# A recommendation-model tower: half grams in two bursts, with transposes and layers between them, and a new order of ScalarE's work

## The chip, the core and the metric

The kernel runs on one core of a Trainium2 chip. Times are device microseconds of one execution of the program; lower is better. The engines of the core work in parallel and wait for one another by semaphores: TensorE (PE; PEld is its weight load), VectorE (DVE), ScalarE (ACT), GpSimd (POOL) and SyncE (SP), which here only issues transfers. DMA engines move the data.

## The reference

A batch of 512 samples looks up 26 embedding rows of 128 numbers each. With the dense vector that makes 27 vectors for each sample. All 351 products of two different vectors, and the dense vector itself, go through three layers.

```python
e = jnp.stack([tbl_0[ids[:, 0]], ..., tbl_25[ids[:, 25]]], axis=1)
T = jnp.concatenate([dense[:, None, :], embs], axis=1)
Z = jnp.einsum('bnd,bmd->bnm', T, T)
z = Z[:, iu0, iu1]                                  # pairs n < m
h = jnp.concatenate([z, r_dense], axis=1)           # 351 + 128 = 479
h = jnp.maximum(h @ W_top1 + b_top1, 0.0)           # 512
h = jnp.maximum(h @ W_top2 + b_top2, 0.0)           # 256
y = h @ W_top3                                      # 1
```

## The kernel before

**Lookups.** Twelve small tables are read whole and looked up on TensorE: for each chunk of 128 table rows a one-hot matrix `hot` (128x512) is made, and two matmuls (with `t_hi`, the table rounded, and `t_lo`, the rest) add the chunk's rows into a PSUM bank. Tables 0 to 5 have 8 chunks and tables 6 to 11 have 10, 108 in all, numbered by k. ScalarE casts `t_hi` (`high_part`), VectorE subtracts for `t_lo` (`low_part`, in the middle of the chunks of the table before). VectorE makes four of five `hot`, ScalarE each fifth (`one_hot`, from `apart`, the distances computed ahead). There are 8 `hot` buffers and three of `t_hi` and `t_lo`: the cast of table i+2 has to wait until TensorE is through with table i-1. ScalarE also copies each finished bank into `XT` (`copy_lookups`). The other 14 fields are gathered row by row by GpSimd (56 gathers, held back by counts of TensorE's progress in `row_turn`), turned on TensorE into two PSUM banks `tp` (steps "rows" t, g; four groups of up to four fields for each tile t) and copied into `XT` by ScalarE.

**Grams.** The batch is cut into four tiles of 128 samples. For each tile there are two half grams of 64 samples: 32 small matmuls (two records each in the trace) into one of two halves of PSUM. VectorE and ScalarE copy each half out: `copy_low` (twice each, into `Zlow`, which lies in `table`'s space) and `copy_high` (twice each, four copies apiece, into `Zt`). The third half has to wait until the first is copied out by both engines (`gram_dve`, `gram_act`), and so on. When both halves of a tile are in `Zlow`, six transfers move parts of it to other partitions of `Zt` (`low_stars`, four of them, and two small ones), and the semaphore `low_in` of the tile tells that they have landed.

**Layers.** "dense" and "layer1" of a tile are 4 and 12 matmuls; layer1 waits for the copies and for `low_in`. VectorE makes `h1` of it, then layer2 follows. Tile 3 is last and has layouts of its own; there GpSimd issues three of the moves.

The order of all of it is written out by hand in `timeline()`. TensorE, ScalarE and VectorE all walk this one list `STEPS`; each takes the kinds that it has work for.

Of the kernel before, what the change touches and what calls it, by code (L numbers as in the profile page):

```python
# [27 lines left out]
P = 128  # L28
BATCH = 512
TILES = BATCH // P  # L30
# [32 lines left out]
ROWS_AFTER = {3: [(0, 0), (0, 1)], 5: [(0, 2), (0, 3)], 7: [(1, 0)], 8: [(1, 1)], 10: [(1, 2)], 11: [(1, 3)]}  # L63
# [16 lines left out]
MOVES = QUADS + SMALL  # L80
SHARED_MOVES = 3
# [19 lines left out]
def timeline():  # L101

    steps = []
    for i in range(K_OH):
        steps.append(("onehot", 0, i))
        steps += [("rows", t, g) for t, g in ROWS_AFTER.get(i, [])]
    steps += [("gram", 0, 0), ("gram", 0, 1), ("rows", 2, 0), ("gram", 1, 0), ("gram", 1, 1), ("rows", 2, 1),
              ("dense", 0, 0), ("layer1", 0, 0), ("layer1", 0, 1), ("rows", 2, 2), ("layer2", 0, 0), ("rows", 2, 3),  # L110
              ("gram", 2, 0), ("gram", 2, 1), ("dense", 1, 0), ("layer1", 1, 0), ("layer1", 1, 1),
              ("rows", 3, 0), ("rows", 3, 1), ("rows", 3, 2), ("dense", 2, 0), ("layer1", 2, 0), ("layer1", 2, 1),
              ("rows", 3, 3), ("gram", 3, 0), ("gram", 3, 1), ("layer2", 1, 0), ("layer2", 2, 0), ("dense", 3, 0),
              ("layer1", 3, 0), ("layer2", 3, 0), ("turn", 0, 0), ("layer3", 3, 0)]
    return steps
# [59 lines left out]
def dlrm_tower(nc, dense, ids, ids_oh, tbls, small, w1, w2, tail, ends, out):  # L175
    f32, f32r, i32 = mybir.dt.float32, mybir.dt.float32r, mybir.dt.int32
    ALU, ACT = mybir.AluOpType, mybir.ActivationFunctionType
    with ExitStack() as ctx:
# [99 lines left out]
        def _(sp):  # L278
# [27 lines left out]
            for t in range(TILES):  # L306
                low_stars(sp, t, range(QUADS - (SHARED_MOVES if t == TILES - 1 else 0)), low_in[t])
# [45 lines left out]
        def _(pe):  # L353
# [14 lines left out]

            pe.wait_ge(ident_ready, 1)
            for _ in range(WARM_UP):  # L370
                nc.tensor.transpose(l1[:, 0, :], ident[:], ident[:])
            for kind, t, i in STEPS:
# [30 lines left out]
                elif kind == "gram":  # L403
# [6 lines left out]
                    if t == 1 and i == 0:  # L410
                        pe.wait_ge(lookup_copied, K_OH)
# [3 lines left out]
                    for q in range(QH):  # L415
                        for s in range(0, SAMPLES, COUPLE):
                            b = t * P + (i * SAMPLES + s) * QH + COUPLE * q
                            last = nc.tensor.matmul(gr[PAD * s:PAD * s + COUPLED, halves % HALVES, q, 0:COUPLE * FIELDS],  # L418
                                                    XT[:, b:b + COUPLE, :].rearrange("d s n -> d (s n)")[:, 0:COUPLED],
                                                    XT[:, b:b + COUPLE, 1:PLACES], start=True, stop=True)  # L420
# [322 lines left out]
```

## Time and profile before

| | before |
|---|---|
| median of 3 runs (lowest to highest) | 116.45 us (116.12 to 116.63) |
| the profiled execution: its time | 116.73 us |
| its span in the trace | 114.9 us |
| busy: PE, PEld, DVE, ACT, POOL | 102.7, 87.2, 79.3, 78.6, 70.4 us |
| shares of the chain that ended last: PE, DMA, SP's queue, issue, DVE, ACT | 58, 9, 9, 9, 8, 6% |

How to read it: the busy time of an engine is a sum over stages, so the share says little by itself. Starts are given from the span's start. For TensorE the distance from start to start is what counts, since its records overlap. A bracket at the end of a row tells how long the engine idled ahead of it and what ended that. The 1.83 us between the execution's time and its span lie outside the trace.

### The profile page before, as it was taken

The page shows a single profiled execution, that of the slowest core. Times are in us where ns is not written, and L with a number is a line of the kernel's source. Part 1 is how long each engine was busy: PE and PEld are TensorE (multiplying, and loading weights), DVE is VectorE, ACT ScalarE, POOL GpSimd, SP SyncE. Part 2 cuts the span into 40 slices and gives each one's busy share as a digit, 9 for nine tenths or more (in the row PEclk, how much of TensorE's full clock was granted, in tenths as well). Part 3 has the DMA queues.
Part 4 walks back from the last instruction along what each step waited for, and adds up shares of the span by engine and source line. Part 5 has one row for each costly group of instructions (what it writes and reads, how often), then busy time and mean ns, then how long its engine had stood idle before and what let it go on. Part 6 is the DMA issues. An engine that isn't in the chain of part 4 may idle for free.

```text
span 114.9 us, 2626 instructions
## 1 busy us (share of the span) xinstructions
PE 102.7 (89%) x981; PEld 87.2 (76%) x981; DVE 79.3 (69%) x202; ACT 78.6 (68%) x169; POOL 70.4 (61%) x68
## 2 busy tenths in 40 slices
PE   4999779999929999999999987897889987899993
PEld 4976456888627888888888877887779976798990
DVE  5497999999196989999999109994227920269531
ACT  4284999999791999999996249998217860168011
POOL 7477786878771377887878776777777600005000
PEclk9999999999995999999999999999999999999999
DMA  2879999998892659982010221232222210000000
GB/s 88 237 263 391 380 382 387 385 328 251 267 273 86 185 200 160 377 282 56 7 39 23 58 56 51 57 86 59 53 70 56 59 36 0 0 6 18 9 0 1
DMA packets 7413, 16.44 MB, mean 143 GB/s; under 512 B 2124, under 2 KB 3048, under 8 KB 7272
## 3 DMA queue, kind: packets, MB, share of 16 engines
q1 hardware_dynamic: 5368, 12.36, 32.7%
q0 software_dynamic: 1888, 3.71, 11.1%
q10 hardware_dynamic: 144, 0.20, 0.5%
q8 instruction: 8, 0.13, 0.5%
q14 instruction: 5, 0.04, 0.1%
HBM read 16.02 MB, written 0.00 MB: 139 GB/s over the span
## 4 chain that ended last, share of the span: by engine, by line
PE 58%; DMA 9%; SPq 9%; issue 9%; DVE 8%; ACT 6%; ACTq 0%; DVEq 0%
PE work L397 17%; PE work L399 17%; PE work L364 6%; DMA ids_bc<-ids_oh 6%; SPq L274 5%; PE work L457 5%; PE work L418 5%; PE tp L383 4%; DMA Zt<-table 3%; DVE Zt L499 3%; DVE table L491 3%; ACT t_hi L512 2%; ACT apart L529 2%; SPq L295 2%; PE work L467 2%
## 5 line engine op out<-in xcount | busy, mean ns | idle before, releaser
L347 POOL DMA_INDIRECT rows<-tbl,idx x56 | 66.7, 1190 | 22.0 <-issue 14.3
L397 PE MATMUL work<-hot,t_hi 128*128 128x512 f32 x108 | 44.1, 408 | 3.9 <-DVE hot L651 3.0
L399 PE MATMUL work<-hot,t_lo 128*128 128x512 f32 x108 | 42.9, 397 | 0.0
L651 DVE TENSOR_SCALAR hot<-ids_bc,rownum 128x512 fp32r<-128x512 int32 x87 | 36.5, 482 | 3.0 <-PE work L399 2.0
L397 PEld LDWEIGHTS work<-hot,t_hi 128*128 128x128 f32 x108 | 20.6, 191 | 11.2 <-DVE hot L651 5.1
L399 PEld LDWEIGHTS work<-hot,t_lo 128*128 128x128 f32 x108 | 20.7, 191 | 3.7
L622 DVE TENSOR_TENSOR t_lo<-table,t_hi 128x1280 fp32r<-128x1280 f32 (+3 forms) x14 | 16.6, 1183 | 4.9 <-ACT t_hi L512 4.6
L593 ACT COPY XT<-tp 128x512 f32<-128x512 f32 (+1 forms) x16 | 9.8, 639 | 12.5 <-PE tp L383 12.5
L529 ACT ACTIVATE apart<-ids_bc,minus_row 128x512 f32<-128x512 int32 x21 | 15.0, 716 | 3.2 <-DMA ids_bc<-ids_oh 3.2
L418 PE MATMUL work<-XT 128*58 128x52 f32 x512 | 14.7, 217 | 2.4 <-DVE Zt L499 1.0
L418 PEld LDWEIGHTS work<-XT 128*58 128x58 f32 x512 | 14.1, 133 | 3.4 <-issue 2.0
L512 ACT CAST t_hi<-table 128x1280 fp32r<-128x1280 f32 (+3 forms) x14 | 14.1, 1009 | 1.7 <-DMA table<-small 1.7
L539 ACT ACTIVATE hot<-apart 128x512 fp32r<-128x512 f32 x21 | 13.3, 636 | 0.9 <-PE work L399 0.8
L499 DVE COPY Zt<-work 17x48 f32<-17x48 f32 (+1 forms) x64 | 12.8, 201 | 1.0
L499 ACT COPY Zt<-work 17x48 f32<-17x48 f32 (+1 forms) x64 | 12.5, 195 | 0.8
L491 DVE COPY table<-work 14x224 f32<-14x224 f32 x16 | 6.1, 381 | 9.3 <-PE work L418 7.3
L551 ACT COPY XT<-work 128x512 f32<-128x512 f32 x11 | 12.2, 1107 | 0.0
L364 PE MATMUL work<-Zt,w_sb 128*128 128x128 f32 x84 | 10.2, 277 | 1.6 <-DMA Zt<-table 1.6
L364 PEld LDWEIGHTS work<-Zt,w_sb 128*128 128x128 f32 x84 | 9.7, 192 | 2.0 <-issue 2.0
L491 ACT COPY table<-work 14x224 f32<-14x224 f32 x16 | 5.7, 356 | 5.8 <-PE work L418 3.4
L274 POOL DMA_DIRECT2D Zt<-table x3 | 1.6, 535 | 12.9 <-DVE table L491 12.9
L383 PE MATMUL tp<-ident,rows 128*128 128x128 f32 x56 | 8.9, 287 | 0.4 <-ACT XT L593 0.4
(44 smaller groups left out, 59.6 us busy)
## 6 DMA issues: line engine op xcount, KB each, us to landing
table<-small SPq DMA_DIRECT2D x6, 640.0 KB, 6.4
ids_bc<-ids_oh SPq DMA_DIRECT2D x12, 256.0 KB, 5.6
table<-small SPq DMA_DIRECT2D x4, 512.0 KB, 9.2
w_sb<-w SPq DMA_DIRECT2D x1, 1024.0 KB, 7.4
rows<-tbl,idx POOLq DMA_INDIRECT x56, 5.5
table<-small SPq DMA_DIRECT2D x2, 320.0 KB, 5.2
w_sb<-w SPq DMA_DIRECT2D x1, 512.0 KB, 8.8
dense_t<-dense SPq DMA_DIRECT2D x1, 256.0 KB, 9.0
```

The lines of the kernel that those rows point to most:

```text
L347: nc.gpsimd.indirect_dma_start(rows[:, t, place - FIRST, :], None, tbls[f], bass.IndirectOffsetOnAxis(ap=idx[:, t, place - FIRST:place - F ...
L364: last = nc.tensor.matmul(l1_block(t, u), w1_sb[:, c, u * P:(u + 1) * P], Zt[:, t, c, :], start=False, stop=c == CHUNKS - 1 and (t == TILE ...
L383: last = nc.tensor.transpose(tp[:, bank, j * P:(j + 1) * P], rows[:, t, a + j - FIRST, :], ident[:])
L397: nc.tensor.matmul(bank, t_hi[:, i % PARTS, c * D:(c + 1) * D], hot[:, k % HOTS, :], start=c == 0, stop=False)
L399: last = nc.tensor.matmul(bank, t_lo[:, i % PARTS, c * D:(c + 1) * D], hot[:, k % HOTS, :], start=False, stop=c == n - 1)
L418: last = nc.tensor.matmul(gr[PAD * s:PAD * s + COUPLED, halves % HALVES, q, 0:COUPLE * FIELDS], XT[:, b:b + COUPLE, :].rearrange("d s n -> ...
L491: return copy(Zlow[:, t % 2, :, first:end:COUPLE], gr[PAD * s:PAD * s + LOW, half, :, column(s):column(s) + LOW].rearrange("n q m -> n m q"))
L499: last = copy(Zt[PAD * g:PAD * g + n, t, :, first:end:COUPLE], gr[PAD * s:PAD * s + n, half, :, column(s) + n - CHUNKS:column(s) + n].rear ...
L512: nc.scalar.copy(t_hi[:, i % PARTS, c0 * D:c1 * D], table[:, i % TABLES, c0 * D:c1 * D]).then_inc(hi_ready, 1)
L529: nc.scalar.activation(apart[:, j % 2, :], ids_bc[:, i % IDS, :], ACT.Abs, bias=minus_row[:, KINDS.index(OH_CHUNKS[i]), c:c + 1]).then_inc ...
L622: nc.vector.tensor_tensor(t_lo[:, i % PARTS, c0 * D:c1 * D], table[:, i % TABLES, c0 * D:c1 * D], t_hi[:, i % PARTS, c0 * D:c1 * D].bitcas ...
L651: nc.vector.tensor_scalar(hot[:, k % HOTS, :], ids_bc[:, i % IDS, :], rownum[:, v, c:c + 1], None, ALU.is_equal).then_inc(hot_dve, 1)
```

## The change

- Each half gram is cut into a "burst" (the first 16 of its matmuls) and "gram" (the other 16, which also tells that the half is full). For tiles 0 to 2, transposes of rows, a tile's dense part, or half a layer1 stand between the two.
- The whole order behind the lookups is new. Rows are turned later among the lookups: one group behind each of tables 4 to 9 instead of up to two behind tables 3, 5, 7, 8, 10 and 11. All of tile 2's rows are turned before tile 1's last half; layer2 of tile 1 stands before tile 3's rows.
- In ScalarE's list the cast of `t_hi` for table i+2 stands first in step i (for tables 0 and 1 behind one `hot`), ahead of the `hot` and the copy of the bank.
- For tiles 0 to 2 two of the four `low_stars` transfers are issued by ScalarE, between its two high copies of the tile's second half; SyncE issues the other two and the two small ones.

```diff
-ROWS_AFTER = {3: [(0, 0), (0, 1)], 5: [(0, 2), (0, 3)], 7: [(1, 0)], 8: [(1, 1)], 10: [(1, 2)], 11: [(1, 3)]}
+ROWS_AFTER = {4: [(0, 0)], 5: [(0, 1)], 6: [(0, 2)], 7: [(0, 3)], 8: [(1, 0)], 9: [(1, 1)]}
+SCALAR_MOVES = 2
...
-                low_stars(sp, t, range(QUADS - (SHARED_MOVES if t == TILES - 1 else 0)), low_in[t])
+                low_stars(sp, t, range(QUADS - (SHARED_MOVES if t == TILES - 1 else SCALAR_MOVES)), low_in[t])
...
+            def couples(t, i, half, first, end):
+
+                for q in range(first, end):
+                    for s in range(0, SAMPLES, COUPLE):
+                        b = t * P + (i * SAMPLES + s) * QH + COUPLE * q
+                        last = nc.tensor.matmul(gr[PAD * s:PAD * s + COUPLED, half, q, 0:COUPLE * FIELDS],
...
-                elif kind == "gram":
+                elif kind == "burst":
                     pe.wait_ge(tp_empty, banks_filled(("rows", t, len(GROUPS) - 1)))
...
+                    couples(t, i, halves % HALVES, 0, QH // 2)
+                elif kind == "gram":
+                    couples(t, i, halves % HALVES, QH // 2, QH).then_inc(gram_full, 1)
                     halves += 1
...
-                    for n, k in enumerate(mine_in(i)[1:]):
+                    rest = mine_in(i)[1:]
+                    if rest and i < HEADED:
+                        one_hot(rest[0])
+                    if i + 2 < K_OH:
+                        high_part(i + 2, 0, OH_CHUNKS[i + 2])
+                    if rest and i >= HEADED:
+                        one_hot(rest[0])
+                    if i:
+                        copy_lookups(i - 1)
+                    for k in rest[1:]:
                         one_hot(k)
...
                     if i + 1 < K_OH:
                         one_hot(mine_in(i + 1)[0])
-                    if i + 2 < K_OH:
-                        high_part(i + 2, 0, OH_CHUNKS[i + 2])
...
+                    if t < TILES - 1 and i == 1:
+                        low_stars(nc.scalar, t, range(QUADS - SCALAR_MOVES, QUADS), low_in[t])
```

ScalarE's list around table 4, before. `table_in5` and `table_in6` mark the casts of tables 5 and 6; the `hot` between them are the eighth of table 4 and the fifth of table 5:

```order
L512 CAST t_hi<-table 128x1024 [waits hot_used,table_in5]
L593 COPY XT<-tp 128x128x4 [waits tp_full] x2
L539 ACTIVATE hot<-apart 128x512 [waits hot_used,apart_ready]
L529 ACTIVATE apart<-ids_bc,minus_row 128x512 [waits hot_act,rownum_ready,ids_in5]
L551 COPY XT<-work 128x512 [waits hot_used]
L539 ACTIVATE hot<-apart 128x512 [waits hot_used,apart_ready]
L529 ACTIVATE apart<-ids_bc,minus_row 128x512 [waits hot_act,rownum_ready,ids_in6]
L512 CAST t_hi<-table 128x1280 [waits hot_used,table_in6]
```

The same place now:

```order
L520 CAST t_hi<-table 128x1280 [waits hot_used,table_in6]
L547 ACTIVATE hot<-apart 128x512 [waits hot_used,apart_ready]
L537 ACTIVATE apart<-ids_bc,minus_row 128x512 [waits hot_act,rownum_ready,ids_in5]
L559 COPY XT<-work 128x512 [waits hot_used]
L547 ACTIVATE hot<-apart 128x512 [waits hot_used,apart_ready]
L537 ACTIVATE apart<-ids_bc,minus_row 128x512 [waits hot_act,rownum_ready,ids_in6]
L606 COPY XT<-tp 128x128x4 [waits tp_full]
L520 CAST t_hi<-table 128x1280 [waits hot_used,table_in7]
```

The cast of table 6 moved ahead of two `hot`, two `apart` and the copy of a bank, and the next cast now stands right behind a copy of turned rows.

TensorE's list behind the last lookup, before:

```order
L418 MATMUL work<-XT 58x52 [waits dense_copied,last_copied,xt_ready,lookup_copied,tp_empty]
L418 MATMUL work<-XT 58x52 x31
L418 MATMUL work<-XT 58x52 [waits tp_empty]
L418 MATMUL work<-XT 58x52 x31
L383 MATMUL tp<-ident,rows 128x128 [waits rows_in2_0,tp_empty]
L383 MATMUL tp<-ident,rows 128x128 x3
L418 MATMUL work<-XT 58x52 [waits gram_dve,gram_act,lookup_copied,tp_empty]
L418 MATMUL work<-XT 58x52 x31
L418 MATMUL work<-XT 58x52 [waits gram_act,gram_dve,tp_empty]
L418 MATMUL work<-XT 58x52 x31
```

And now, from the burst of tile 0's second half to the burst of tile 1's second:

```order
L377 MATMUL work<-XT 58x52 x16
L361 MATMUL work<-dense_t,w1_sb 128x128 [waits dense_in,w1_in,lookup_copied]
L361 MATMUL work<-dense_t,w1_sb 128x128 x3
L377 MATMUL work<-XT 58x52 [waits gram_act,gram_dve,tp_empty]
L377 MATMUL work<-XT 58x52 x15
L396 MATMUL tp<-ident,rows 128x128 [waits rows_in2_1,tp_empty]
L396 MATMUL tp<-ident,rows 128x128 x3
L377 MATMUL work<-XT 58x52 x16
L396 MATMUL tp<-ident,rows 128x128 [waits rows_in2_2,tp_empty]
L396 MATMUL tp<-ident,rows 128x128 x3
L377 MATMUL work<-XT 58x52 [waits gram_act,gram_dve,tp_empty]
L377 MATMUL work<-XT 58x52 x15
```

The dense part and the groups of rows moved in between the halves and into them; the fourth half still waits for the second to be copied out.

ScalarE's list at tile 0's second half gram, before (`table` is `Zlow`):

```order
L491 COPY table<-work 14x14x16 x2
L499 COPY Zt<-work 17x3x16
L499 COPY Zt<-work 20x3x16
L499 COPY Zt<-work 23x3x16
L499 COPY Zt<-work 26x3x16
```

and now, with the two copies of turned rows that stand ahead of it and the two transfers behind the first high copy:

```order
L606 COPY XT<-tp 128x128x2
L606 COPY XT<-tp 128x128x4
L499 COPY table<-work 14x14x16 x2
L507 COPY Zt<-work 17x3x16
L507 COPY Zt<-work 20x3x16
L507 COPY Zt<-work 23x3x16
L507 COPY Zt<-work 26x3x16
L277 DMA Zt<-table 8x384
L277 DMA Zt<-table 5x384
```

The second high copy, four more copies, moved behind two issues.

## Rows read from the trace of the kernel before

**Rows 1.** Timeline of TensorE around table 5's end: start, duration, instruction, [idle before].

```profile
33.74 0.66 PE L397 MATMUL work<-hot,t_hi 128*128 128x512 f32 x1 [2.21 <-DVE hot L651]
...
37.40 0.48 PE L397 MATMUL work<-hot,t_hi 128*128 128x512 f32 x1
```

**Rows 2.** Timeline of ScalarE and VectorE ahead of that.

```profile
30.51 1.25 ACT L512 CAST t_hi<-table 128x1280 fp32r<-128x1280 f32 x1
...
31.79 1.49 DVE L622 TENSOR_TENSOR t_lo<-table,t_hi 128x1280 fp32r<-128x1280 f32 x1 [2.57 <-ACT t_hi L512]
```

**Rows 3.** Busy times by stretch: the granted clock (PEclk) behind that gap.

```profile
core 0: us, PE busy (x) PEld busy (x) DVE busy (x) ACT busy (x) POOL busy (x), PEclk, DMA share, GB/s
...
33.00:36.00 3.00, 2.26 (x6) 1.78 (x7) 2.66 (x7) 1.89 (x3) 1.19 (x1) 0.65 0.69 262
```

**Rows 4.** Timeline of TensorE: table 8's first and seventh chunk, table 9's first.

```profile
46.94 0.48 PE L397 MATMUL work<-hot,t_hi 128*128 128x512 f32 x1
...
49.77 0.39 PE L397 MATMUL work<-hot,t_hi 128*128 128x512 f32 x1
...
51.95 0.48 PE L397 MATMUL work<-hot,t_hi 128*128 128x512 f32 x1
```

**Rows 5.** Timeline of ScalarE in the same place.

```profile
46.15 1.25 ACT L512 CAST t_hi<-table 128x1280 fp32r<-128x1280 f32 x1
47.31 0.71 ACT L593 COPY XT<-tp 128x512 f32<-128x512 f32 x1
47.89 0.62 ACT L539 ACTIVATE hot<-apart 128x512 fp32r<-128x512 f32 x1
```

**Rows 6.** DMA issues from 12.4 to 12.8 us (table 6): size, us to landing.

```profile
table<-small SPq DMA_DIRECT2D x1, 640.0 KB, 9.9
```

**Rows 7.** Timeline of GpSimd's gathers where one waits for TensorE.

```profile
39.74 1.16 POOL L347 DMA_INDIRECT rows<-tbl,idx  x1 [1.87 <-PE work L399]
```

**Rows 8.** Timeline of TensorE behind the lookups.

```profile
66.92 3.62 PE L418 MATMUL work<-XT 128*58 128x52 f32 x128 [0.43 <-issue]
70.47 0.66 PE L383 MATMUL tp<-ident,rows 128*128 128x128 f32 x4
...
82.14 1.97 PE L457 MATMUL work<-w_sb,apart 128*128 128x256 f32 x8 [0.44 <-issue]
83.94 0.38 PE L383 MATMUL tp<-ident,rows 128*128 128x128 f32 x2
...
88.34 1.16 PE L358 MATMUL work<-dense_t,w_sb 128*128 128x128 f32 x8
89.33 2.84 PE L364 MATMUL work<-Zt,w_sb 128*128 128x128 f32 x24
92.01 1.04 PE L383 MATMUL tp<-ident,rows 128*128 128x128 f32 x8
...
99.34 3.62 PE L418 MATMUL work<-XT 128*58 128x52 f32 x128 [0.47 <-ACT XT L593]
...
107.49 1.57 PE L364 MATMUL tp<-Zt,w_sb 128*128 128x128 f32 x12
```

**Rows 9.** Timeline of ScalarE: its copies of the first half gram.

```profile
68.93 0.74 ACT L491 COPY table<-work 14x224 f32<-14x224 f32 x2 [1.35 <-PE work L418]
69.70 1.64 ACT L499 COPY Zt<-work 17x48 f32<-17x48 f32 x8
```

**Rows 10.** The chain that ended last, from 90 to 95.7 us: start, us, what.

```profile
90.16 0.83 SPq L274
...
91.86 0.66 SPq L274
...
92.57 0.71 SPq L274
...
93.91 1.69 DMA Zt<-table
```

**Rows 11.** Timeline of SyncE's issues for tile 3.

```profile
103.83 0.83 SPq L274 DMA_DIRECT2D Zt<-table  x1
104.71 1.17 SPq L309 DMA_DIRECT2D Zt<-table  x2
```

**Rows 12.** Timeline of the first issues on two queues.

```profile
0.74 0.38 ACTq L553 DMA_DIRECT2D table<-small  x1
...
0.74 0.42 SPq L286 DMA_DIRECT2D idx<-ids  x1
```

More of the change, by code:

```diff
@@ L108, in timeline @@
         steps += [("rows", t, g) for t, g in ROWS_AFTER.get(i, [])]
[L109 to L114, printed above, removed]
+    steps += [("burst", 0, 0), ("rows", 1, 2), ("gram", 0, 0), ("rows", 1, 3), ("burst", 0, 1), ("rows", 2, 0),
+              ("gram", 0, 1), ("dense", 0, 0), ("burst", 1, 0), ("rows", 2, 1), ("gram", 1, 0), ("rows", 2, 2),
+              ("burst", 1, 1), ("rows", 2, 3), ("gram", 1, 1), ("layer1", 0, 0), ("layer1", 0, 1), ("layer2", 0, 0),
+              ("burst", 2, 0), ("dense", 1, 0), ("gram", 2, 0), ("layer1", 1, 0), ("burst", 2, 1), ("layer1", 1, 1),
+              ("gram", 2, 1), ("layer2", 1, 0), ("rows", 3, 0), ("rows", 3, 1), ("dense", 2, 0), ("rows", 3, 2),
+              ("layer1", 2, 0), ("layer1", 2, 1), ("rows", 3, 3), ("burst", 3, 0), ("gram", 3, 0), ("burst", 3, 1),
+              ("gram", 3, 1), ("layer2", 2, 0), ("dense", 3, 0), ("layer1", 3, 0), ("layer2", 3, 0), ("turn", 0, 0),
+              ("layer3", 3, 0)]
     return steps
@@ L367, in from_pairs @@
                 return last
+            def couples(t, i, half, first, end):
[3 more added lines that the diff above has]
+                        last = nc.tensor.matmul(gr[PAD * s:PAD * s + COUPLED, half, q, 0:COUPLE * FIELDS],
+                                                XT[:, b:b + COUPLE, :].rearrange("d s n -> d (s n)")[:, 0:COUPLED],
+                                                XT[:, b:b + COUPLE, 1:PLACES], start=True, stop=True)
+                return last
             pe.wait_ge(ident_ready, 1)
@@ L409, in _ @@
                         pe.wait_ge(xt_ready, 1)
-                    if t == 1 and i == 0:
-                        pe.wait_ge(lookup_copied, K_OH)
                     if halves >= HALVES:
@@ L414, in _ @@
                         pe.wait_ge(gram_act, halves - HALVES + 1)
[L415 to L420, printed above, removed]
-                    last.then_inc(gram_full, 1)
+                    couples(t, i, halves % HALVES, 0, QH // 2)
+                elif kind == "gram":
+                    couples(t, i, halves % HALVES, QH // 2, QH).then_inc(gram_full, 1)
                     halves += 1
@@ L424, in _ @@
                     if t == 0:
+                        pe.wait_ge(lookup_copied, K_OH)
                         pe.wait_ge(w1_in, 16)
@@ L562, in _ @@
                 if kind == "onehot":
-                    for n, k in enumerate(mine_in(i)[1:]):
+                    rest = mine_in(i)[1:]
[8 more added lines that the diff above has]
+                    for k in rest[1:]:
                         one_hot(k)
-                        if n == 0 and i:
-                            copy_lookups(i - 1)
-                    if i and len(mine_in(i)) < 2:
-                        copy_lookups(i - 1)
                     if i + 1 < K_OH:
                         one_hot(mine_in(i + 1)[0])
-                    if i + 2 < K_OH:
-                        high_part(i + 2, 0, OH_CHUNKS[i + 2])
                     if i == K_OH - 1:
```

## The prediction

> **What bounds the kernel now.** I read the page first (TensorE has by far the most busy time), then TensorE's timeline for its gaps, then the timelines of the engines that ended them, and the chain that ended last for the stretch behind the lookups. TensorE runs nearly without a break from 19 to 66 us, except once: it idles 2.21 us ahead of table 5's sixth chunk [rows 1]. VectorE had waited 2.57 us for the cast of table 6 before it could go on to `t_lo` and that chunk's `hot`; ScalarE only began the cast at 30.51 [rows 2]. Behind the gap the granted clock is 0.65 over 33 to 36 us [rows 3], so part of that stretch ran at the lower of TensorE's two levels (1.2 instead of 2.4 GHz) after the engine had idled. Behind the lookups TensorE alternates grams, transposes and layers with gaps under 1 us, each set by a copy or by the moves into `Zt`.
>
> **The gap among the lookups goes.** In the new list the cast of table 6 waits only for TensorE to end table 3 (24.5 us) and for the table itself, issued at 12.4 and 9.9 us later there, at 22.3 [rows 6]. So it ends near 26.2, before VectorE wants it (near 28.9). What the gap cost: TensorE would have issued the next matmul at 31.37 and did at 33.74, 2.37 us. From there to 37.40 are 3.66 us [rows 1] for three chunks and six transposes. A table of ten chunks with four transposes takes 5.01 us [rows 4] and four transposes about 0.45 (70.47 to the end of a group in rows 8; eight are 1.04 busy), so a chunk is 0.456 and the stretch should be 1.37 + 0.66 = 2.03 us: 1.63 lost at the low level. Together 4.0 us.
>
> **Two things take part of it back.** First, with the transposes behind table 3 gone, TensorE wants table 4's sixth chunk sooner, and VectorE, which has just made a `t_lo`, is about 0.25 us late. Second, ScalarE now does, behind each of tables 5 to 9: copy of the turned rows, cast, then the `hot` of the next table's seventh chunk. By rows 5 that is 0.58 + 1.16 + 0.62 from a start at 0.37 behind the table's first matmul (47.31 against 46.94): ready at 2.73. The chunk's matmul starts at 49.77 - 46.94 = 2.83 [rows 4, 5], its weight load 0.2 ahead. That is no slack at all; I take 0.1 us for each of five tables. So the same work among the lookups ends 4.0 - 0.25 - 0.5 = 3.25 us sooner. One group of transposes (0.45) also moves behind the lookups: the last lookup ends at 62.3 and not at 66.06, and the first burst starts at 63.15 instead of 66.92 [rows 8]. GpSimd's gathers follow: the one that waited 1.87 us for TensorE [rows 7] waits for table 6's first group of chunks, now near 34.8, so all later gathers shift some 3.8 us with it and the rows are there in time.
>
> **Behind the lookups.** Prices [rows 8], start to start: a half gram 3.55 / 2 = 1.78, so a burst 0.9; four transposes 0.45, two 0.22; dense 1.0 (88.34 to 89.33); layer1 2.68 (to 92.01), half of it 1.35; layer2 1.8 (82.14 to 83.94). ScalarE's copies of a half take 0.77 + 1.64 = 2.4 us and start 0.2 behind its last matmul [rows 9]; a copy of turned rows is 0.6 [rows 5].
> ScalarE's walk: half (0,0) is full at 65.4 and copied at 68.0; two row copies to 68.9; half (0,1): low until 69.7, first high until 70.5, then the second high has to wait for the two issues.
> *Price of an issue on ScalarE.* The trace has none behind compute. The same two transfers cost SyncE 0.66 and 0.71 with 0.04 between [rows 10], 1.42 in all. Lower bound: they are hidden, 0. Upper: nothing is hidden, 1.45. They only wait for the low copies, and four high copies (0.82, half of rows 9) stand between; I take it that the queue issues while these run, so 0.65 is exposed. That lies near the middle, and both ends stay in the range.
> So (0,1) is copied at 72.0. TensorE, from 63.15: burst, 4 transposes, gram, 2 transposes, burst, 4 transposes, gram, dense (68.9), burst, 4, gram, 4 (71.6); the burst of (1,1) waits for ScalarE until 72.1; burst, 2 transposes, gram (74.15). Tile 0's moves: SyncE now has four issues instead of six, which takes 1.45 from the 5.44 us between the low copy's end and landing (90.16 to 95.60 [rows 10]): 69.75 + 4.0 = 73.75, in time. Layer1 of tile 0 to 76.85; `h1` costs 1.04 with no cover any more (rows (2,2) filled 0.45 of it); layer2 to 79.7. Then burst, dense, gram, half layer1, burst, half layer1, gram: 7.3, to 87.0; layer2 of tile 1 to 88.95; 8 transposes and dense to 90.85; 4 transposes, 91.35. Tile 2's moves: low copies end 88.0, landed 92.0. Layer1 of tile 2 from 92.15 to 94.85, where it was 95.74 + 2.7 before. Two transposes and their copy, 0.9: tile 3's grams start at 95.75 instead of 99.34. Change: 3.6 us.
>
> **Tile 3.** Before, 8.15 us from there to layer1 (107.49) [rows 8], filled by two layer2. Now one of them (1.8) has gone ahead, but that gives nothing: tile 3's moves are issued at 103.83 and 104.71 for 1.17 [rows 11]; the last of them starts near 105.3 and lands no sooner than the 1.7 us of rows 10 later, at 107.0, so layer1 can't start before 7.7 us after the grams. TensorE will idle about 1.8 us there: the gap that layer2 covered comes open. I keep 8.15; 7.7 would be 0.4 less.
>
> **Sum.** 3.6 us sooner, less 0.3 for a dozen more changes of the kind of work on TensorE, which rows 8 show to cost little but not nothing: 3.3. On the profiled execution 116.73 - 3.3 = 113.4; the median of the runs is 0.28 below it, so **113.2 us**. Its own range is 112.5 to 114.1.
>
> **A rule on the issues.** The Trainium skill, Perfetto Trace Analysis, section DMA Instruction — HWDGE (DVE, Sync), says that the block that generates descriptors is shared and locked for exclusive use during an issue. By it SyncE's and ScalarE's issues would queue behind one another, and the first rival below would come out, at 115.7. But two queues issue at the same moment, in 0.38 and 0.42 us [rows 12], each no longer than alone, which speaks against it for these sizes.
>
> **Rivals.**
> - *ScalarE's issues take turns with SyncE's.* ScalarE is then held for four issues, about 2.85 us instead of 1.42. (0,1) is copied at 73.4, the burst of (1,1) starts 1.4 later; the six issues are in one row again, tile 2's moves land 5.44 and not 4.0 behind the low copies. Sum: 1.4 + 1.4 of the 3.6 are lost: 116.45 - 0.8 = 115.7. Against it: [rows 12]. 12%.
> - *The issues on ScalarE are hidden.* Another 0.65 off, and up to 0.4 in tile 3: 112.3. 13%.
> - *The clock falls again.* TensorE idles 1.8 us before the last layer1 and about 1 us in three other places. 2.21 us of idling went ahead of a fall [rows 1, 3], gaps of 0.4 did not [rows 8]; between them nothing is known. Price as above, 1.63: 114.8. 14%.
> - *Slower than before: ScalarE's list becomes the bound in the lookups.* Rows copy, cast and `hot` are a closed loop with TensorE (the transposes at a table's end release the copy). I gave it 0.1 us a table. If the `hot` comes 0.75 late in each of five tables, 3.3 us are gone and the kernel is at 116.5 or above; a fall of the clock in such gaps would do it at less. For: the loop has no slack. Against: its parts are all measured, 2.73 against 2.83. 8%; within 0.5% by a partial miss 5%.
> - The forecast 48%.
>
> Range: from the hidden issues to the shared generator, **112.1 to 115.7**. A measurement can tell about 0.5% (0.6 us) from no change: faster by more 0.86, within it 0.06, slower 0.08.
>
> **What would show it.** TensorE without a gap over 0.5 us between 20 and 62, the granted clock at full there, the last lookup's end near 62.3; ScalarE's second high copy starting 0.6 us behind the first in half (0,1); layer1 of tile 2 near 92; tile 3's grams near 96 and its layer1 8 us later with TensorE idle ahead of it. Wrong if a new gap ahead of each table's seventh chunk stands in TensorE's timeline, if ScalarE's issues are longer than 0.75 us, or if the clock is low behind 90 us.

## The result, and the profile after

| | before | after |
|---|---|---|
| median (lowest to highest), 4 runs each | 116.28 us (116.03 to 116.63) | 115.09 us (114.55 to 115.36) |
| the profiled execution: time, span | 116.73, 114.9 us | 115.36, 113.6 us |
| first half gram of tile 0 starts | 66.92 | 62.07 |
| tile 3's grams start | 99.34 | 97.98 |

The ratio is 0.989 (95% interval 0.984 to 0.994): 1.2 us faster, where 3.3 were forecast. A ratio with an interval, here and below, leaves out the slower runs of a kernel where enough fast ones are there, so it can differ from the ratio of the medians, which are of all runs. Read by its landmarks the change has three pieces: the first half gram starts 4.85 us sooner, the way from there to tile 3's grams is 3.49 us longer (35.91 against 32.42), and the rest is the same (15.62 against 15.56). 4.85 - 3.49 - 0.06 = 1.3 us of span.

**The lookups.** TensorE's timeline, with the only idle time over 0.1 us between 20 and 62 us, the first half gram, and the stretches of the window view:

```profile
34.94 0.50 PE L410 MATMUL work<-hot,t_hi 128*128 128x512 f32 x1 [0.21 <-ACT hot L547]
62.07 1.06 PE L377 MATMUL work<-XT 128*58 128x52 f32 x32 [0.62 <-issue]
```

```profile
core 0: us, PE busy (x) PEld busy (x) DVE busy (x) ACT busy (x) POOL busy (x), PEclk, DMA share, GB/s
25.00:62.00 37.00, 36.24 (x169) 28.94 (x167) 32.30 (x65) 33.33 (x49) 30.60 (x22) 1.00 0.58 174
62.07:97.98 35.91, 32.70 (x531) 28.90 (x531) 17.87 (x69) 19.88 (x71) 20.96 (x23) 1.00 0.19 50
97.98:113.60 15.62, 11.94 (x189) 10.62 (x189) 7.02 (x29) 5.36 (x23) 1.58 (x3) 1.00 0.03 6
```

The gap of [rows 1] is gone. The 0.21 us that are left stand elsewhere, ahead of table 6's seventh chunk, whose `hot` ScalarE makes: of the five tables for which I had given such a chunk 0.1 us each, only this one waits. The granted clock is full (1.00, 2.4 GHz), where [rows 3] had 0.65.

**Behind the lookups.** TensorE's timeline from the first burst on (a matmul of a gram leaves two records, so a burst of 16 is x32):

```profile
63.06 0.66 PE L396 MATMUL tp<-ident,rows 128*128 128x128 f32 x4
63.65 1.06 PE L377 MATMUL work<-XT 128*58 128x52 f32 x32
64.64 0.44 PE L396 MATMUL tp<-ident,rows 128*128 128x128 f32 x2
65.01 1.06 PE L377 MATMUL work<-XT 128*58 128x52 f32 x32
...
70.24 1.06 PE L377 MATMUL work<-XT 128*58 128x52 f32 x32
71.58 0.63 PE L396 MATMUL tp<-ident,rows 128*128 128x128 f32 x4 [0.28 <-issue]
72.14 1.06 PE L377 MATMUL work<-XT 128*58 128x52 f32 x32
74.04 0.41 PE L396 MATMUL tp<-ident,rows 128*128 128x128 f32 x2 [0.84 <-DMA rows<-tbl,idx]
```

From start to start a burst is 0.99 (62.07 to 63.06), where I took 0.9, four transposes are 0.59 and not 0.45, two are 0.37 and not 0.22. And at 71.58 and 74.04 TensorE waits for rows (the trace names no releaser for the first; in d1 below, where the rows are always there, that wait is absent too): the chain that ended last runs through GpSimd's gathers, with the last of them here:

```profile
70.05 0.95 POOL rows L350
71.00 0.30 issue
71.30 2.60 DMA rows<-tbl,idx
74.04 0.41 PE tp L396 x2
```

The gather issued at 71.30 was issued at 73.04 before. It came 1.74 us sooner, not 3.8. In GpSimd's timeline of before these two rows are the other wait for TensorE beside the one of [rows 7], and that gather:

```profile
36.80 1.07 POOL L347 DMA_INDIRECT rows<-tbl,idx  x1 [2.60 <-PE work L399]
...
73.04 0.94 POOL L347 DMA_INDIRECT rows<-tbl,idx  x1 [0.30 <-issue]
```

Both waits are gone after, and no gather waits more than 0.31 us any more from 20 to 86 us. But GpSimd itself has become later, not only TensorE sooner: its 8th to 30th gathers start later than before. The first row here is the 15th, the longest; the other two are the 20th, after and before:

```profile
28.17 3.47 POOL L350 DMA_INDIRECT rows<-tbl,idx  x1 [0.30 <-issue]
37.88 2.28 POOL L350 DMA_INDIRECT rows<-tbl,idx  x1 [0.30 <-issue]
```

```profile
33.01 1.19 POOL L347 DMA_INDIRECT rows<-tbl,idx  x1 [0.30 <-issue]
```

So GpSimd is 4.87 us late there by longer gathers. From the 34th to the 54th gather each takes 1.25 us from start to start in both kernels, and the lead over before stays at 1.7 us. Why the gathers among the tables take longer is not shown: the share of the DMA engines from 28 to 32 us is 0.82, and was 0.88 before.

**The moves on ScalarE.** The timelines of ScalarE and SyncE, tiles 0 and 1:

```profile
69.04 1.23 ACTq L277 DMA_DIRECT2D Zt<-table  x1
70.30 0.75 ACTq L277 DMA_DIRECT2D Zt<-table  x1
71.10 0.83 ACT L507 COPY Zt<-work 17x48 f32<-17x48 f32 x4 [1.28 <-issue]
...
76.87 0.69 ACTq L277 DMA_DIRECT2D Zt<-table  x1
77.59 0.72 ACTq L277 DMA_DIRECT2D Zt<-table  x1
```

```profile
69.05 1.79 SPq L277 DMA_DIRECT2D Zt<-table  x2
...
76.85 1.66 SPq L277 DMA_DIRECT2D Zt<-table  x2
```

The two issue at the same time: four transfers in 2.0 us (69.04 to 71.05) and in 1.66 us, where taking turns at [rows 10]'s 0.7 would be 2.85. They start right behind the low copies while the first high copies run, as assumed; the exposed part is 1.28 us for tile 0 and about 0.7 for the others, where I took 0.65. The issue of 1.23 us is longer than the 0.75 that the prediction gave as a sign of being wrong; it is the only one of ScalarE's six. The rule of the Trainium skill (Perfetto Trace Analysis, section DMA Instruction — HWDGE (DVE, Sync)) of an exclusive lock, taken over whole issues, is not what these rows show; a lock over a part of each they can't rule out, and the 1.23 beside 0.7 speaks of some contention.

**Tile 2's layer1 and tile 3.**

```profile
94.38 2.92 PE L367 MATMUL work<-Zt,w_sb 128*128 128x128 f32 x24 [0.47 <-DMA Zt<-table]
...
97.98 3.62 PE L377 MATMUL work<-XT 128*58 128x52 f32 x128 [0.47 <-ACT XT L606]
...
106.14 1.13 PE L367 MATMUL tp<-Zt,w_sb 128*128 128x128 f32 x8 [1.72 <-DMA Zt<-table]
```

Tile 3 came out as forecast: 8.16 us from its grams to its layer1 (8.15), with 1.72 us idle (1.8) in the place that layer2 of tile 1 had filled.

### The profile page after: what moved, and what is told of

Its sections match the earlier page's. It is cut to its first block, busy times and chain, and to the rows that moved or that the text cites. A ratio compares the mean times of both kernels' runs of the same rounds, so it can differ in the third digit from the quotient of the medians.

```text
span 113.6 us, 2628 instructions
## 1 busy us (share of the span) xinstructions
PE 103.5 (91%) x981; PEld 86.6 (76%) x981; DVE 78.7 (69%) x202; ACT 78.4 (69%) x169; POOL 72.7 (64%) x68
## 4 chain that ended last, share of the span: by engine, by line
PE 42%; ACT 16%; issue 12%; DMA 10%; POOL 10%; DVE 4%; SPq 4%; ACTq 0%; DVEq 0%; POOLq 0%
PE work L410 10%; POOL rows L350 10%; PE work L412 10%; PE work L367 9%; PE work L377 6%; ACT hot L547 5%; DMA table<-small 4%; ACT XT L559 4%; DMA Zt<-table 3%; ACT apart L537 3%; ACT t_hi L520 3%; DMA rows<-tbl,idx 2%; SPq L277 2%; DVE table L499 2%; PE tp L396 2%
## 5 line engine op out<-in xcount | busy, mean ns | idle before, releaser
L350 POOL DMA_INDIRECT rows<-tbl,idx x56 | 68.9, 1230 | 20.1 <-issue 15.2
L412 PE MATMUL work<-hot,t_lo 128*128 128x512 f32 x108 | 42.2, 391 | 0.0
L377 PEld LDWEIGHTS work<-XT 128*58 128x58 f32 x512 | 14.7, 133 | 3.5 <-issue 2.4
L377 PE MATMUL work<-XT 128*58 128x52 f32 x512 | 16.4, 218 | 1.1 <-issue 0.6
L507 DVE COPY Zt<-work 17x48 f32<-17x48 f32 (+1 forms) x64 | 12.8, 200 | 1.0
L559 ACT COPY XT<-work 128x512 f32<-128x512 f32 x11 | 12.4, 1128 | 0.0
```

What stands on the lines that cost most here:

```text
L350: nc.gpsimd.indirect_dma_start(rows[:, t, place - FIRST, :], None, tbls[f], bass.IndirectOffsetOnAxis(ap=idx[:, t, place - FIRST:place - F ...
L377: last = nc.tensor.matmul(gr[PAD * s:PAD * s + COUPLED, half, q, 0:COUPLE * FIELDS], XT[:, b:b + COUPLE, :].rearrange("d s n -> d (s n)")[ ...
L412: last = nc.tensor.matmul(bank, t_lo[:, i % PARTS, c * D:(c + 1) * D], hot[:, k % HOTS, :], start=False, stop=c == n - 1)
L507: last = copy(Zt[PAD * g:PAD * g + n, t, :, first:end:COUPLE], gr[PAD * s:PAD * s + n, half, :, column(s) + n - CHUNKS:column(s) + n].rear ...
L559: nc.scalar.copy(XT[:, :, 1 + i], lookup_bank(i)).then_inc(lookup_copied, 1)
```

## The experiments

The chips matter here. In four of the five series (chips 3, 7, 5 and 6) the kernel before takes 124 to 126 us. It has no trace there, but in the trace of every other kernel on these chips TensorE stops inside the small gram matmuls, also in those that have its order (a1, b1, e1); in the first comparison and on chip 11 no trace has such stops. So a kernel's time is compared with kernels of its own chip alone. The series are told in order.

### First series: one part at a time (chip 3; the kernel before 124.95 us)

a1 is the kernel before with ScalarE's new list. a4 is the changed kernel with the old list, a2 has each half gram in one piece, a3 has all moves on SyncE:

```diff
-("burst", 0, 0), ("rows", 1, 2), ("gram", 0, 0), ("rows", 1, 3), ("burst", 0, 1), ("rows", 2, 0), ("gram", 0, 1)
+("burst", 0, 0), ("gram", 0, 0), ("rows", 1, 2), ("rows", 1, 3), ("burst", 0, 1), ("gram", 0, 1), ("rows", 2, 0)   # a2
...
-SCALAR_MOVES = 2
+SCALAR_MOVES = 0   # a3
```

> The kernel before with one part of the change: ScalarE's casts first, everything else as before. My theory now: the change won 4.85 us among the lookups (first half gram at 62.07 instead of 66.92) and lost 3.5 us between there and tile 3's grams (35.91 instead of 32.42 us). So this kernel keeps most of the gain and pays none of the loss: first half gram near 63, tile 3's grams 32.4 to 33 us later, time 112.3 to 113.0. Rival (gathers): the gathers of GpSimd do not follow when TensorE runs ahead, so the tail stretches here too by 1 us or more: 113.5 to 114.5, with TensorE waiting for rows. Rival (the later turns of rows made the gain): first half gram still near 66.

> The changed kernel with each half gram of tiles 0 to 2 in one piece again; what stood between its two bursts now stands behind it. Theory (changes of kind): each extra change between small gram matmuls and other work costs TensorE 0.1 to 0.2 us, some 2 us in all over 12 pieces; unsplit, the stretch from the first half gram to tile 3's grams falls from 35.9 to 34 us and the time to about 113.2. Rival (gathers): the stretch is long because rows of tile 2 land late (waits of 0.28 and 0.84 us); unsplit leaves them: 114.5 to 115.3.

> The changed kernel with all moves of tiles 0 to 2 issued by SyncE again. If the two moves on ScalarE pay by landing tile 2's moves earlier (4.25 us behind the low copies instead of 5.4), this is slower by about 1.1 us: 116.2. Rival: what they hold up on ScalarE (1.28, 0.72 and 0.76 us idle ahead of the second high copy) and the slower issues beside SyncE's were the loss; then this is faster: 114.4.

> The changed kernel with ScalarE's old list (cast last in each step). The gap ahead of the sixth chunk of table 5 comes back with VectorE waiting for the cast of table 6. If the parts add up, the 4 us of the gap and of the low clock return: 118.5 to 119.5. If the later turns of rows already close part of the gap (a copy of turned rows no longer stands ahead of the cast), less: 116.5 to 118.

Measured: a1 124.52 us, ratio 1.013 (0.999 to 1.027); a2 129.9, 1.055 (1.030 to 1.081); a3 130.88, 1.060 (1.041 to 1.079); a4 128.71, 1.045 (1.039 to 1.051). The landmarks still tell something of the lookups: the first half gram is at 62.57 in a1, so the list alone closes the gap (one of 0.50 us is left), and at 63.52 in a4, whose largest gap is 1.72 us and after which the granted clock stays full: the later turns of rows shorten the gap too. The times tell nothing of the first comparison, for behind 62 us all four kernels stop again and again.

### Second series: the same on another chip (chip 7; the kernel before 123.81 us)

b1, b2 and b3 repeat a1, a2 and a3. b5 is a1 with two moves of tiles 0 to 2 on ScalarE:

```diff
+                    if t < TILES - 1 and i == 1:
+                        low_stars(nc.scalar, t, range(QUADS - SCALAR_MOVES, QUADS), low_in[t])
```

> The same kernel as in the first series (the kernel before with ScalarE's casts first). There TensorE stopped 0.3 to 1.1 us again and again inside the small gram matmuls with nothing that it waited for, and the kernel before took 125 instead of 116 us; so the tail could not be compared. Without such stops: first half gram near 62.6 as there, tile 3's grams 32.4 to 33 us later, 112.0 to 113.0. If the gathers hold the tail: 113.5 to 114.5.

> The changed kernel with its half grams in one piece. Theory (changes of kind cost TensorE): stretch from the first half gram to tile 3's grams near 34 us, time 113.2. Theory (late gathers): 35 us or more, 114.5 to 115.3.

> The changed kernel with all moves on SyncE. If the moves on ScalarE pay: 116.2. If what they hold up was the loss: 114.4.

> The kernel before with ScalarE's casts first and the two moves on ScalarE, without the new order of the tail. The waits of TensorE for moves that have to land (0.86 and 0.78 us before) shrink by about 1 us each, at 0.7 us of delay on ScalarE's second high copy, which nothing in this order waits for at once except the first gram of tile 2: 111.5 to 112.5. Rival: tile 1's grams and ScalarE's copies are late by the issues and the gain is eaten: as without the moves, 112.5 to 113.

Measured: b1 123.92, level with before; b2 131.36, ratio 1.057 (1.047 to 1.067); b3 132.39, 1.055 (1.045 to 1.066); b5 122.34, 0.986 (0.980 to 0.992). The kernel before spreads from 120.28 to 126.38 us over its thirteen runs here, and its fastest is below all four of b5 (122.06 to 122.89), so b5's 1.4% is no sure win. The stops are not of one chip, and there the kernels with the old order behind the lookups do better than those with the new one.

### Third series: the changed kernel, the stops, the price of a change of kind (chip 5; the kernel before 125.21 us)

c1 is the changed kernel. c2 is b5's with its warm-up matmuls altered so that the code behind them shifts. c3 has four extra transposes of the identity behind each of tile 3's four gram pieces, c4 all 16 behind the last:

```diff
-("burst", 3, 0), ("gram", 3, 0), ("burst", 3, 1), ("gram", 3, 1)
+("burst", 3, 0), ("fill", 0, 0), ("gram", 3, 0), ("fill", 0, 1), ("burst", 3, 1), ("fill", 0, 2), ("gram", 3, 1), ("fill", 0, 3)   # c3
+("burst", 3, 0), ("gram", 3, 0), ("burst", 3, 1), ("gram", 3, 1), ("fill", 0, 0), ("fill", 0, 1), ("fill", 0, 2), ("fill", 0, 3)   # c4
```

> The changed kernel itself, beside the kernel before, in the setting of the two series so far (kernel before at 124 to 125 us, TensorE stopping for 0.3 to 1.1 us with no releaser inside the half grams of tile 0). Theory A: the new order behind the lookups is what loses there, since its bursts and short turns run into the same stops as the kernels that kept that order (4 to 6% slower than before). Then this one takes 128 to 131 us, ratio 1.03 to 1.06, although it was 0.989 in the first comparison. Theory B: each of the earlier kernels lost by the part it had taken out, and the change as a whole wins here too: 121 to 123.5 us, ratio 0.98 to 0.995. If the kernel before comes back at 116 us, the setting has gone, and the ratio should be 0.985 to 0.995 by both.

> The kernel with ScalarE's new list and two moves on ScalarE (0.986 in the second series), with TensorE's warm-up of 24 transposes turned into 16 transposes and 16 matmuls of two columns, so that every later matmul stands 8 places (16 records with its weight load, 24 less 8) further on in TensorE's code at nearly the same time. Theory: the stops inside the small gram matmuls are tied to a place in the code (they began 44 to 50 records into the first half gram in every kernel so far); then the first stop moves to some 20 to 35 records into it. Rival: they are tied to the work itself (the read of XT, the PSUM banks written, the copies beside it); then the first stop stays at 44 to 50 records. The time by both is within 1 us of the unshifted kernel's 122.3. If the setting has gone and there are no stops, it tells nothing of either.

> The changed kernel with four extra transposes of the identity behind each of tile 3's four gram pieces (16 in all, into a PSUM tile that nobody reads), to price a change between small gram matmuls and transposes by the difference to the next kernel, which issues all 16 behind the last piece. Theory (a change of kind costs): tile 3's gram and filler stretch is 0.6 to 0.9 us longer here than there, over six more changes of kind, 0.10 to 0.15 us each. Rival (changes cost nothing, what the bursts take longer in the changed kernel is something else): the two stretches agree within 0.15 us.

> The changed kernel with the same 16 extra transposes in one row behind tile 3's last gram piece. The pair of the kernel ahead: from the start of tile 3's grams to the end of the last filler 3.6 us for the grams plus some 1.8 us for 16 transposes, 5.4 us, if a change of kind costs only once; the kernel ahead takes 6.0 to 6.3 us by the theory and 5.4 us by the rival.

c1: 129.54 us against 125.21, every run of it above every run of before (128.97 against 126.44 at the nearest). The same program that won by 1.1% on the first chip loses by 3.5% here (medians of all runs). That is the time of theory A; that short bursts make the stops worse is not shown by it. TensorE's timeline in c1, where the first chip had no idle time at all:

```profile
62.05 1.06 PE L377 MATMUL work<-XT 128*58 128x52 f32 x32 [0.62 <-issue]
63.05 0.65 PE L396 MATMUL tp<-ident,rows 128*128 128x128 f32 x4
63.63 0.85 PE L377 MATMUL work<-XT 128*58 128x52 f32 x18
65.56 0.33 PE L377 MATMUL work<-XT 128*58 128x52 f32 x5 [1.08 <-issue]
67.00 0.32 PE L377 MATMUL work<-XT 128*58 128x52 f32 x4 [1.11 <-issue]
68.42 0.47 PE L377 MATMUL work<-XT 128*58 128x52 f32 x5 [1.09 <-issue]
```

The engine waits for no semaphore that the profile shows ("issue"), does four or five records, and stops for another 1.1 us. The granted clock follows, in c1's window view:

```profile
65.00:70.00 5.00, 1.25 (x15) 0.76 0.20 56
70.00:75.00 5.00, 4.43 (x66) 0.56 0.10 26
```

Its DMA view shows one packet (0.02 MB; the eight of this queue have 0.13, so 16 KB each) in the queue called "instruction" at 69.2 to 70.0 us, where the stops nearly end; the changed kernel on the first chip has the packet of this place at 64.4 to 65.2 us, in time:

```profile
q8 instruction: 1, 0.02, 7.9%
```

c2 (124.84 us, one run; within 1 us of 122.3 was expected, from another chip): its first stop comes 51 records into the first half gram, not 20 to 35. So the stops are not tied to a place in the code that I shifted, as far as one run tells. In all kernels with unbroken half grams and stops the first stop comes 44 to 51 records into the run of small matmuls, and a later run often stops after 44 to 49; in those with bursts it comes after 50 such records, with four transposes between them. That looks like a store of instructions that runs out when matmuls of 31 ns follow one another. It stays an inference. The Trainium skill (Advanced Engine Details and Errata, section ISA Cache) gives blocks of 16 KB or 256 instructions, which the size of the packets agrees with. That crossing a block is mostly hidden (Runtime: NRT & Kernel Launch, section Instruction fetch mechanics) agrees with the first comparison and chip 11; on the four others it would not hold, if the stops are the fetch.

c3 and c4: from tile 3's grams to the end of the fillers, read at layer2's start, in the two timelines:

```profile
111.74 1.06 PE L377 MATMUL work<-XT 128*58 128x52 f32 x32 [0.47 <-ACT XT L609]
...
117.97 1.25 PE L468 MATMUL work<-w_sb,apart 128*128 128x256 f32 x5
```

```profile
112.89 3.62 PE L377 MATMUL work<-XT 128*58 128x52 f32 x128 [0.47 <-ACT XT L609]
...
118.25 1.03 PE L468 MATMUL work<-w_sb,apart 128*128 128x256 f32 x4
```

6.23 us against 5.36 for the same matmuls, over six more changes between grams and transposes: 0.87 us, inside the 0.6 to 0.9 expected, **0.145 us each**. No stop falls into either stretch and the granted clock is 1.00 in both. It is one profile of each kernel (their times, 131.36 and 130.31 us, are of single runs); but c3's pieces are those of the changed kernel in the first comparison: 0.99 us for a burst and 0.59 for four transposes, against 0.89 and 0.45 in c4's unbroken rows.

### Fourth series: half the gathers (chip 11; the kernel before 114.69 us)

d1 is the changed kernel, d2 the unsplit one, d3 the kernel before, d4 that with the new list alone. In all four the gathers of tiles 2 and 3 are left out, and their transposes read the rows of tiles 0 and 1:

```diff
-            for t in range(TILES):
+            for t in range(2):
...
-                    pe.wait_ge(rows_in[t][i], 16 * n)
+                    pe.wait_ge(rows_in[t % 2][i], 16 * n)
```

> The changed kernel, with the gathers of tiles 2 and 3 left out (their transposes read the rows of tiles 0 and 1 again, so the outputs of two tiles are other numbers, and GpSimd gathers 28 times instead of 56 and is done near 55 us). Theory G: the stops inside the small gram matmuls, which in every kernel of the three series ended once the last gathers were done (last stop at 93.6 to 97.4 us, tile 3's grams never stopped), come from the gathers at work beside TensorE's own fetch of instructions. Then there are no stops, and with the wait for rows gone too (1.1 us in the changed kernel's profile) it takes 113.5 to 115 us. Rival: the stops come from TensorE's fetch alone; then they stay, some 12 us of them, and it takes 126 us or more.

> The kernel ahead with each half gram of tiles 0 to 2 in one piece, so that TensorE changes its kind of work 22 times instead of 30 between the first half gram and tile 3's. If changes at 0.145 us (last series: 6 extra ones cost 0.87) are what the bursts cost, 1.2 us are saved by that, and what the bursts covered comes back as waits for the copies: within 1 us of the kernel ahead, either way. If the bursts cover more than they cost it is slower by over 1 us. With the stops still there it tells little.

> The kernel before, with the gathers of tiles 2 and 3 left out in the same way. Theory G: no stops, 115.5 to 117 us, and the changed kernel with half the gathers stands 2 to 3 us (1.7 to 2.6%) under it: the first comparison's 1.2 us and the 1.1 us of late rows on top. Rival: with stops 123 to 125 us. The gap behind table 5 stays (2.2 us, and with it the low granted clock) since ScalarE's list is the old one.

> The kernel before with ScalarE's new list alone, with half the gathers. By the changed kernel's profile the lookups end 4.4 us sooner with the new list; the rest of the program is as before, so theory G gives 111.5 to 113 us, under the changed kernel with half the gathers: the new order behind the lookups then gives nothing or takes 1 to 2 us. If the order behind the lookups gains by itself, the changed kernel is the faster of the two. Rival, with stops: 122 us or more.

| | d1 changed | d2 unsplit | d3 before | d4 list alone |
|---|---|---|---|---|
| median us (lowest to highest) | 114.38 (114.04 to 114.75) | 115.88 (115.41 to 116.24) | 115.35 (113.69 to 116.60) | 112.58 (112.13 to 113.05) |
| first half gram | 62.08 | 62.74 | 64.39 | 62.64 |
| to tile 3's grams | 34.96 | 36.03 | 32.42 | 32.10 |
| from there to the end of the span | 15.56 | 15.63 | 15.59 | 15.56 |

No kernel stops here, but neither does the kernel before with all its gathers (114.69), so theory G is neither borne out nor refuted. The chip is like the first one in this, and the four can be compared. Against the kernel before with all its gathers their ratios are 1.000 (0.996 to 1.004), 1.013 (1.002 to 1.025), 1.004 (0.996 to 1.011) and 0.987 (0.975 to 0.999). The window view of TensorE over the second line's stretch, for d1, d2 and d4:

```profile
62.08:97.04 34.96, 32.69 (x530) 1.00 0.04 8
```

```profile
62.74:98.77 36.03, 30.85 (x531) 1.00 0.03 7
```

```profile
62.64:94.74 32.10, 28.00 (x517) 1.00 0.04 8
```

- **Late rows cost 0.95 us**: the changed kernel needs 35.91 us with all gathers (on the first chip) and 34.96 when the rows are always there. The idle times agree: the waits of 0.28 and 0.84 us are gone, and the burst of tile 1's second half waits 0.16 us for ScalarE's copy instead, at 72.06. That is the 72.1 of the prediction by luck: the first burst is 1.07 us sooner than forecast, and the way from it 1.0 us longer.
- **The bursts gain in this order**: without them the stretch is 1.07 us longer (d2 against d1) and the kernel 1.5 us, so the expectation's second case, over 1 us, came out. d2 is busy for 1.84 us less (30.85 against 32.69), but idles 5.2 instead of 2.3 us: 1.96 us for ScalarE's copies of turned rows in three places, and 1.9 us for VectorE's `h1` ahead of tile 1's layer2, which in d2's list stands right behind its layer1, where the changed kernel has a gram between them. A list with unsplit half grams and something in that place was not run, so this part may be the place and not the split. One wait of each kind in d2:

```profile
67.91 0.66 PE L396 MATMUL tp<-ident,rows 128*128 128x128 f32 x4 [0.61 <-ACT XT L606]
...
91.23 1.97 PE L465 MATMUL work<-w_sb,apart 128*128 128x256 f32 x8 [1.89 <-DVE apart L690]
```

- **The new order gains nothing**: with the same list, the stretch takes 2.86 us longer than in the old order (34.96 against 32.10). Of this some 2.5 is work moved in (at the prediction's prices: layer2 of tile 1 1.8, six transposes 0.67), and the tail from which layer2 came is no shorter (15.56 and 15.56). The order saves 1.8 us of idling (4.10 to 2.27) and spends 2.2 us on its work's own being longer (busy time up 4.69, less the 2.5). The whole kernel is 1.8 us slower than d4. For d4 the expectation held (112.58 in 111.5 to 113, under the changed kernel).
- **The expectation for d3 against d1 missed**: 1.0 us apart, not 2 to 3. The reason is the clock. The kernel's gap is as before, but in d3's profiled run the granted clock does not fall behind it, in the windows of TensorE:

```profile
32.87 0.50 PE L397 MATMUL work<-hot,t_hi 128*128 128x512 f32 x1 [2.21 <-DVE hot L651]
```

```profile
33.00:36.00 3.00, 3.00 (x17) 1.00 0.47 172
36.00:39.00 3.00, 3.00 (x15) 1.00 0.79 263
```

Of d3's ten runs three have a mean granted clock of 1.0 (113.69 to 114.21 us) and seven one of 0.985 (115.16 to 116.60 us, median 115.46). The mean of 0.985 is that of the profile of the kernel before, with its one fall; none of the seven has a profile, so where their clock fell is not seen. Against the 113.74 of the three that is 1.7 us. The two profiles say the same: from the gap's end to the first half gram are 31.52 us in d3 (32.87 to 64.39) and 33.18 in the kernel before (33.74 to 66.92), 1.66 us for one fall of the clock, where the prediction had 1.63. The kernel before, which has the gap too, has the 0.985 in 7 of its 19 runs on this chip; d1, d2 and d4, whose largest gap in the lookups is 0.5 us or less, in none of 18. The gain from closing the gap is so 1.2 us when the clock would have held and 2.9 us when it would have fallen (d4, 112.58).

This bears on the first comparison. Its 1.2 us are less than one fall costs, and the profile of the kernel before has a fall. Here the changed kernel (d1, 114.38) is 1.1 us under d3 where d3's clock fell and 0.6 us above it where it held. So the first comparison's win is likely the fall that it avoids; no run there with a full clock in the kernel before shows it.

### Fifth series: the list alone and with the moves, all gathers (chip 6; the kernel before 125.95 us)

e1 and e2 are the programs of a1 and b5.

> The kernel before with ScalarE's new list and nothing else, all gathers in, on a chip where TensorE doesn't stop inside the small matmuls (if it is such a one). Half the gathers gave 112.58 against 115.35 us for the old list. The old order behind the lookups wants the rows later than the new one, so all the gathers should cost it at most 1 us: 112.5 to 114 us, ratio to the kernel before 0.975 to 0.99, and first half gram to tile 3's grams 32.0 to 33.0 us against 35.9 in the changed kernel. Rival: the late rows cost here what they cost there or more, and it is no better than the changed kernel (ratio 0.99 or above). If TensorE stops here as in the first three series, 121 to 125 us and a ratio of 1.0 to 1.01 as twice before.

> The kernel before with ScalarE's new list and two of tile 0's to 2's moves on ScalarE, without the new order on TensorE. The moves shorten the wait for the rows of Zt by up to 1.4 us per tile where TensorE waits for it (0.55 ahead of tile 0's layer1 and 0.77 ahead of tile 2's in the trace with half the gathers), and lengthen ScalarE's copy of a half by 0.65 to 1.3 us ahead of the next gram. I expect 0.3 to 1.0 us less than the kernel ahead: 112 to 113.5 us, ratio 0.97 to 0.985. Rival: ScalarE's copy is what TensorE waits for next, and it is the same as the kernel ahead within 0.3 us or slower.

Measured: 125.45 us, ratio 1.005 (0.998 to 1.011), and 125.99, 1.003 (0.994 to 1.012). This is again a chip with stops (nine in e1 from 66 to 75 us), so the clean measurement of the list alone with all gathers is missing, and b5's win of 1.4% did not repeat. In e1's trace TensorE also waits 1.29 us for rows at 49 us, among the lookups; the same program had no such wait in a1 and b1, but with all gathers the list alone isn't safe from late rows. What the two moves on ScalarE are worth is open as well: with them 1.6 us less on chip 7 (b5 against b1) and 0.5 us more here. On such chips little done in the lookups shows in the time: 62.75 us for the first half gram in e2 ends in the same 126 us.

## Why the prediction was wrong

Two steps failed, both behind the lookups: the term of 0.3 us for changes of the kind of work, which was 2.4, and the gathers that were to follow TensorE.

- **The gap among the lookups goes**: right. The new list alone brings it from 2.21 to 0.5 us or less (a1, b1, d4), and the low clock was worth what was taken (1.66 measured, 1.63 forecast).
- **Two things take part of it back** (0.25 late, 0.1 for each of five tables): too much. The first half gram is at 62.07, not 63.15, with one gap of 0.21 us. Of these 1.08 us 0.75 is what I had taken back; for the other 0.33 no run shows the source.
- **Gathers "shift some 3.8 us with it and the rows are there in time"**: this step failed. They shifted by 1.74 us, and the rows were late by 0.28 and 0.84 us. I had moved GpSimd's work by the length of its wait and not asked what it would meet instead: longer gathers among the table loads, and then its own 1.25 us a gather.
- **"Less 0.3 for a dozen more changes of the kind of work"**: this step failed by most. I had priced a burst as half of a half gram of [rows 8], which has no seam in it, and so with the rest. Piece by piece in the timeline after, start to start, up to tile 3's grams: twelve bursts are 0.99 and not 0.9 each (1.1 us in all), six groups of transposes 3.02 and not 2.24, two halves of a layer1 1.53 and not 1.35 each, two dense parts 1.08 and not 1.0. Together 2.4 us. The price from c3 and c4 agrees: the old order changes its kind of work 16 times on this way and the new one 30 times, and 14 times 0.145 is 2.0 us, an estimate, since only changes between grams and transposes were measured.
- **The sum of that stretch**: forecast 32.6, measured 35.91. The 3.31 us too little are 2.4 of longer pieces (0.3 of it allowed for in the sum), 0.6 of waits (1.12 for late rows, where 0.5 for ScalarE was forecast), and 0.28 at 93.25 for the copy of tile 3's turned rows.
- **The exposed 0.65 of the issues, and no taking of turns**: right for tiles 1 and 2, low for tile 0 (1.28), which shows on TensorE only as the 0.16 us of d1. The rival at 115.7 did not come about by its mechanism, though the time is near it. Its sum had left out the 0.3 for changes; with it it would have been 115.95.
- **Tile 3**: right, 8.16 for 8.15 and the gap that layer2 had covered came open.
- **The clock falls again**: no. Idle times up to 1.72 us here (94 to 113 us), 1.72 us in a4's lookups and 1.89 us in d2 went by with the clock at full.

By size: 1.08 better in the lookups, 3.31 - 0.3 worse behind them, 0.06 in the tail, which makes 2.0 of 113.6 - 111.6 us of span. That the time still lies within 2 us of the forecast is luck in part: the first of these errors took back a third of the second.

## What to carry to other kernels

Price interleaved work with the change of kind that each piece brings (0.145 us here between small matmuls and transposes): splitting a stretch pays only where the idle time that it fills is larger, and moving work out of a stretch that waits for a transfer gives nothing. When a wait of a feeding engine goes, ask what it meets next before shifting all its work. Do the part that gains by itself as a kernel of its own: here, with half the gathers, the new list alone stood 1.8 us under list and order together. And read the granted clock of each run before crediting a gain of 1% to the order of the work: one fall was worth 1.7 us here.

## What was not expected of the hardware

- One program, two orders of merit: the changed kernel is 1.1% faster than before on one chip and 3.5% slower on another, where TensorE stops 0.4 to 1.1 us at a time inside runs of small matmuls. Whether these stops come from the fetch of its code, and why on four chips and not on the others, is open. The gathers beside it were not ruled out: the last stop is at 94 to 99 us and the last gather starts at 96 to 106, and tile 3's grams, behind both, never stopped. But on chip 11 the kernel before ran without the loss with all its gathers.
- With the same 2.21 us of idling the mean granted clock was 0.985 in seven of ten runs of one kernel and 1.0 in three; one of the three has a profile, and there the clock held through the gap.
